# Causal attention with experts on one core: masked scores in two buffers, outputs in four, softmax inverses spread in fp32

## What is computed

```
xn = layernorm(x)
Q, K, V = heads(xn @ W_qkv)                 # 16 heads of 64
Q, K = rope on the first 32 of the 64 dims
scores = Q K^T, masked above the diagonal, / 8
attn = softmax(scores)
out = x + (attn V) @ W_o + experts(xn)      # top 2 of 8 experts and a skip; gelu between two products
```

## Time and profile before

| | us |
|---|---|
| median of 3 runs | 1490.87 (1490.24 to 1496.87) |
| the profiled execution | 1500.74, span 1499.0 |
| attention of the former samples, in the span | from about 128 to 690 |
| attention of the latter samples | from about 935 to the end |
| busy, share of the span | PE 84%, DVE 80%, ACT 75%, POOL 57% |

### The profile page before, as it was taken

How to read it: one execution, slowest core, us unless ns; L and a number is a source line. 1 busy time by engine, 2 the same in 40 slices (tenths; PEclk the granted TensorE clock), 3 DMA queues, 4 the chain that set the end, 5 groups by cost and what they waited for, 6 DMA issues and landing times.

```text
span 1499.0 us, 46446 instructions
## 1 busy us (share of the span) xinstructions
PE 1254.0 (84%) x15156; PEld 940.5 (63%) x15157; DVE 1195.7 (80%) x4018; ACT 1122.6 (75%) x3606; POOL 858.6 (57%) x1194
## 2 busy tenths in 40 slices
PE   1416999888888898895999999888888889888888
PEld 1404666666666666664889898566666666666666
DVE  5788877777777887783777777889988889889886
ACT  6415888877787787784878887878777777777786
POOL 3254777777777777773000000767777777666775
PEclk9757999999999999997999999999999999999999
DMA  9621433333333333333232322333333333333330
GB/s 290 204 56 38 101 73 73 74 72 72 74 72 74 72 80 79 75 83 111 72 88 84 87 84 75 77 80 79 80 82 92 91 84 80 89 91 89 85 80 27
DMA packets 115831, 130.12 MB, mean 87 GB/s; under 512 B 11568, under 2 KB 75312, under 8 KB 115376
## 3 DMA queue, kind: packets, MB, share of 16 engines
q1 hardware_dynamic: 107056, 110.26, 30.6%
q0 software_dynamic: 8576, 17.33, 3.8%
HBM read 28.85 MB, written 31.59 MB: 40 GB/s over the span
## 4 chain that ended last, share of the span: by engine, by line
PE 28%; DVE 22%; DMA 17%; POOL 16%; issue 13%; ACT 4%; POOLq 0%; DVEq 0%; SPq 0%; ACTq 0%
DMA sorted_x_dram<-stage,slots 17%; PE bank L1102 6%; PE bank L1103 6%; PE bank L1104 6%; DVE arena L956 4%; POOL sorted_x_dram L497 3%; POOL arena L476 3%; PE bank L1173 3%; DVE arena L919 2%; DVE arena L918 2%; POOL arena L456 2%; PE bank L1184 2%; POOL arena L457 2%; ACT probs L643 2%; PE bank L1211 2%
## 5 line engine op out<-in xcount | busy, mean ns | idle before, releaser
L643 ACT ACTIVATE probs<-arena,neg_max 128x128 f32<-128x128 f32 (+1 forms) x1024 | 452.3, 446 | 110.5 <-DVE neg_max L956 108.5
L956 DVE CUSTOM_DVE_ANT_0 arena<-bank,causal 128x128 f32<-128x128 f32 (+1 forms) x1024 | 302.3, 349 | 46.6 <-PE bank L1173 46.1
L507 POOL DMA_INDIRECT stage<-sorted_y_dram,slots x128 | 130.5, 1020 | 257.9 <-DVE arena L919 238.6
L1184 PE MATMUL bank<-ident,probs 128*128 128x128 f32 x1536 | 212.6, 275 | 13.5 <-ACT probsT L626 10.7
L633 ACT ACTIVATE o_whole<-bank 128x256 f32<-128x256 f32 x256 | 97.7, 382 | 151.5 <-PE bank L1195 85.2
L497 POOL DMA_INDIRECT sorted_x_dram<-stage,slots x128 | 133.3, 1041 | 128.6 <-DMA sorted_x_dram<-stage,slots 104.2
L1184 PEld LDWEIGHTS bank<-ident,probs 128*128 128x128 f32 x1536 | 177.2, 142 | 39.6 <-issue 18.4
L643 ACT ACTIVATION_READ_ACCUMULATOR probs<-arena,neg_max 128x1 f32 x1024 | 194.7, 190 | 0.0
L1102 PE MATMUL bank<-arena 128*128 (+1 forms) x864 | 183.2, 238 | 1.5 <-DVE arena L1076 1.5
L476 POOL TENSOR_TENSOR arena<-o_whole,arena 128x256 f16<-128x256 f32 x256 | 172.0, 672 | 21.0
L1103 PE MATMUL bank<-arena 128*128 (+1 forms) x864 | 182.7, 238 | 0.0
(11 more groups left out here) (152 smaller groups left out, 3258.8 us busy)
## 6 DMA issues: line engine op xcount, KB each, us to landing
arena<-arena SPq DMA_DIRECT2D x256, 256.0 KB, 3.8
arena<-sorted_x_dram SPq DMA_DIRECT2D x72, 128.0 KB, 2.2
sorted_y_dram<-stage SPq DMA_DIRECT2D x72, 128.0 KB, 1.8
sorted_x_dram<-arena SPq DMA_DIRECT2D x3, 2304.0 KB, 17.8
arena<-experts_dram SPq DMA_DIRECT2D x8, 512.0 KB, 5.6
out_dram<-acc SPq DMA_DIRECT2D x32, 128.0 KB
sorted_x_dram<-arena SPq DMA_DIRECT2D x1, 2368.0 KB, 19.1
sorted_x_dram<-stage,slots POOLq DMA_INDIRECT x128, 2.5
```

The costliest lines, as they stand in the source:

```text
L643: last = nc.scalar.activation(probs[:, s % 4, at:at + w], masked[:, s % 4, at:at + w], ACT.Exp, bias=neg_max[:, s % 4, t:t + 1], scale=-1. ...
L956: last = nc.vector.tensor_tensor_reduce(out=masked[:, (s + i) % 4, at:at + w], in0=SC[i][:, at:at + w], in1=causal[:, at:at + w], scale=1. ...
L1184: last = nc.tensor.transpose(TP[s % 2][:, k * P:(k + 1) * P], probs[:, s % 4, k * P:(k + 1) * P], ident[:])
```

## The change

- masked has two buffers, one for each head of a pair; the masks of a head wait until the exponentials of the same head of the pair before are done.
- o_whole has four buffers instead of two. o_copy waits for the products with v (pv_done) and for the split of the output four pairs back.
- invert runs once a pair and is a reciprocal alone; the row sums have four buffers instead of eight. turn_sums spreads the fp32 reciprocals by products with the fp32 identity, one for each row tile and head, and runs one period earlier (PV_LAG), after the units and before the transposes. The wait for o_scaled moves from attend to it. The factor 64 of the fp16 parts is gone.
- In the samples that have AHEAD units, except samples 0 and 16, "rest 0" of the sample after next moves from period 5 to the head of period 3, and within a period the units are ordered by table alone: AHEAD, then USUAL, then VALUES. So in period 7 "rest 1" comes before "v_low 1".

```diff
-AHEAD = ((5, "rest", 0), (6, "rope", 0), (7, "rest", 1))
+AHEAD = ((3, "rest", 0), (6, "rope", 0), (7, "rest", 1))
+AHEAD_OPENING = ((5, "rest", 0), (6, "rope", 0), (7, "rest", 1))
...
-T_LAG, PV_LAG, OUT_LAG, INV_LAG, SPLIT_LAG, BACK_LAG = 1, 2, 2, 3, 4, 2
+T_LAG, PV_LAG, OUT_LAG, COPY_LAG, SPLIT_LAG, BACK_LAG = 1, 2, 2, 3, 4, 2
-QUAD = 4
-SUMS = 2 * QUAD
+SUMS = 4
+OUTPUTS = 4
...
-    steps = [(p, kind, j, b if kind == "v_high" else b - 1 if kind == "y" else b + 1)
-             for p, kind, j in (OPENERS if b in (0, MID) else USUAL) if nearer or kind in ("v_high", "y")]
-    steps += [(p, kind, j, b + 2) for p, kind, j in AHEAD if further]
+    opening = b in (0, MID)
+    steps = [(p, kind, j, b + 2) for p, kind, j in (AHEAD_OPENING if opening else AHEAD) if further]
+    steps += [(p, kind, j, b if kind == "v_high" else b - 1 if kind == "y" else b + 1)
+              for p, kind, j in (OPENERS if opening else USUAL) if nearer or kind in ("v_high", "y")]
     steps += [(p, kind, j, b + 1) for p, kind, j in VALUES if nearer]
-    return sorted(steps, key=lambda step: (step[0], step[1] == "rest" or step[0] == 6 and step[1] == "v_low"))
+    return sorted(steps, key=lambda step: step[0])
...
-            pool.wait_ge(made, MADE - 1)
-            nc.gpsimd.tensor_copy(ident_h[:], ident[:]).then_inc(made, 1)
...
             def o_copy(J, j):
-                act.wait_ge(inv_turned, J + 1)
-                if not (isinstance(J, int) and J < 2):
-                    act.wait_ge(o_done, J - 1)
-                nc.scalar.activation(o_whole[:, j % 2, :], PV[j % 2], ACT.Copy).then_inc(o_out, 1)
+                act.wait_ge(pv_done, 2 * J + 2)
+                if J >= OUTPUTS:
+                    act.wait_ge(o_done, J - OUTPUTS + 1)
+                nc.scalar.activation(o_whole[:, J % OUTPUTS, :], PV[j % 2], ACT.Copy).then_inc(o_out, 1)
...
             def masks(b, s):
                 dve.wait_ge(s_ready, 8 * b + s // 2 + 1)
-                if not (b == 0 and s < 4):
-                    dve.wait_ge(exp_done, 16 * b + s - 2)
                 for i in range(2):
+                    if b > 0 or s > 0:
+                        dve.wait_ge(exp_done, 16 * b + s + i - 1)
...
-            def invert(N, n):
-                dve.wait_ge(exp_done, QUAD * N + QUAD)
...
+            def invert(J):
+                dve.wait_ge(exp_done, 2 * J + 2)
+                if J >= 2:
+                    dve.wait_ge(inv_turned, J - 1)
+                of = slice(J % 2 * 2, J % 2 * 2 + 2)
+                nc.vector.reciprocal(inv_total[:, of, :], total[:, of, :]).then_inc(inv_done, 1)
...
-                nc.vector.scalar_tensor_tensor(o_whole[:, j % 2, :], INV[j % 2], UNSCALE, o_whole[:, j % 2, :],
-                                               ALU.mult, ALU.mult).then_inc(o_scaled, 1)
+                nc.vector.tensor_tensor(o_whole[:, J % OUTPUTS, :], INV[j % 2], o_whole[:, J % OUTPUTS, :], ALU.mult).then_inc(o_scaled, 1)
...
-            def turn_sums(b, j):
...
+            def turn_sums(b, j, at):
+                pe.wait_ge(inv_done, 8 * b + j + 1)
                 if at == REOPEN and j == 0:
                     pe.wait_ge(y2_done, TILES)
                 if not (at == OPENING and j < 2):
                     pe.wait_ge(o_scaled, 8 * b + j - 1)
+                for t in range(TPS):
+                    for i in range(2):
+                        of = inv_total[:, j % 2 * 2 + i, t:t + 1].broadcast_to([P, DK])
+                        last = mm(INV[j % 2][64 * i:64 * i + 64, t * P:(t + 1) * P], of, ident[:], start=True, stop=True)
+                last.then_inc(inv_turned, 1)
...
             def sample(b, parity, at):
                 for p in range(PAIRS):
                     scores(b, 2 * p, parity, at == OPENING)
-                    then = past(b, p, INV_LAG)
-                    if then:
-                        turn_sums(*then)
                     for kind, j, of, u, psum in units_at(b, p):
                         unit(kind, j, of, of % 2, psum, bank_free(u))
+                    ended = past(b, p, PV_LAG)
+                    if ended:
+                        turn_sums(*ended, at)
                     then = past(b, p, T_LAG)
                     if then:
                         transposes(*then, then[0] == 0)
-                    then = past(b, p, PV_LAG)
-                    if then:
-                        attend(*then, at)
+                    if ended:
+                        attend(*ended)
```

More of the change, by code:

```diff
@@ L168, in attention_and_experts @@
         probs = sb("probs", [P, 4, PW], F32)
-        masked = view(MASKS, 4 * PW).rearrange("p (i n) -> p i n", i=4)
+        masked = view(MASKS, 2 * PW).rearrange("p (i n) -> p i n", i=2)
         probsT = sb("probsT", [P, 4, PW], F32)
@@ L173, in attention_and_experts @@
         inv_total = sb("inv_total", [P, SUMS, TPS], F32)
-        inv_parts = sb("inv_parts", [P, 2, SUMS, TPS], F16)
-        ident_h = sb("ident_h", [P, P], F16)
-        o_whole = sb("o_whole", [P, 2, SEQ], F32)
+        o_whole = sb("o_whole", [P, OUTPUTS, SEQ], F32)
         rot_q, rot_k = (view(ROT + i * 512, 2 * SEQ).rearrange("p (f t) -> p f t", f=2) for i in range(2))
@@ L220, in attention_and_experts @@
             "s_ready", "s_masked", "exp_done", "inv_done", "t_ready", "pv_done"))
-        inv_hi, inv_ready, inv_turned = (sem(n) for n in ("inv_hi", "inv_ready", "inv_turned"))
+        inv_turned = sem("inv_turned")
         t_out = [sem("t_out_dve"), sem("t_out_act")]
@@ L235, in attention_and_experts @@
         block = ctx.enter_context(nc.Block())
-        MADE = 7
+        MADE = 6
         ZEROED = 3 + E + 1 + 3
@@ L639, in exps @@
                     act.wait_ge(t_ready, G - 3)
-                if not (at_first and s < SUMS) and s % QUAD == 0:
-                    act.wait_ge(inv_done, G // QUAD - 1)
+                if G >= SUMS and s % 2 == 0:
+                    act.wait_ge(inv_done, G // 2 - 1)
                 for t, (at, w) in enumerate(((0, P), (P, 2 * P))):
-                    last = nc.scalar.activation(probs[:, s % 4, at:at + w], masked[:, s % 4, at:at + w], ACT.Exp,
+                    last = nc.scalar.activation(probs[:, s % 4, at:at + w], masked[:, s % 2, at:at + w], ACT.Exp,
                                                 bias=neg_max[:, s % 4, t:t + 1], scale=-1.0,
@@ L652, in sample @@
                     turned(past(b, p, OUT_LAG))
-                    then = past(b, p, INV_LAG)
+                    then = past(b, p, COPY_LAG)
                     if then:
@@ L1013, in sample @@
                     masks(b, 2 * p)
+                    then = past(b, p, 1)
+                    if then:
+                        invert(8 * then[0] + then[1])
                     for kind, j, of, u, psum in units_at(b, p):
@@ L1016, in sample @@
                             turn(j, u, psum, of)
-                    then = past(b, p, INV_LAG)
+                    then = past(b, p, COPY_LAG)
                     if then:
                         o_scale(8 * then[0] + then[1], then[1])
-                    then = past(b, p, 2)
-                    if then and p % 2 == 0:
-                        invert(4 * then[0] + then[1] // 2, then[1] // 2)
                     for kind, j, of, u, psum in due(b, p, 2):
@@ L1185, in transposes @@
                     last.then_inc(t_ready, 1)
-            def turn_sums(b, j):
-                if j % 2 == 0:
-                    pe.wait_ge(inv_ready, 4 * b + j // 2 + 1)
-                for t in range(TPS):
-                    for l in range(2):
-                        for i in range(2):
-                            of = inv_parts[:, l, 2 * j % SUMS + i, t:t + 1].broadcast_to([P, DK])
-                            last = mm(INV[j % 2][64 * i:64 * i + 64, t * P:(t + 1) * P], of, ident_h[:], start=(l == 0), stop=(l == 1))
-                last.then_inc(inv_turned, 1)
-            def attend(b, j, at):
-                if j % 4 == 0:
-                    pe.wait_ge(v_ready, 4 * b + (2 if j == 0 else 4))
+            def turn_sums(b, j, at):
+                pe.wait_ge(inv_done, 8 * b + j + 1)
                 if at == REOPEN and j == 0:
```

32 lines of the change are left out of this document (12 added, 20 removed).

## The result

The changed kernel takes 1615.3 us (median of 4 runs, 1607.61 to 1619.67) beside 1491.7 us of the kernel before on the same chip: ratio 1.0816, 95% interval 1.0767 to 1.0866. It is slower by 124 us where 25 were forecast, and the time lies outside the range (1478 to 1540 us). The profiled execution's span went from 1499.0 to 1612.2 us.

What follows compares the result with a forecast made beforehand. No engine was full: GpSimd's chain bound the former stage, a chain mostly through VectorE the latter. Ring +28.6 us in moved samples, less 3 us in unmoved, net +25.6 on 1490.9 gave 1516 us; range 1478 to 1540 us.

Steps and rivals of the forecast that it cites:

- the mask buffers: Two buffers for masked scores: forecast to cost nothing, at most 0.5 us in a few periods; rival that they bind, 0.05.
- the inverses' waits: Latter stage: waits on the inverses' fp16 parts (TensorE, 12.1 us in four samples) and before the output copy would go.
- the ring: Loop from q stack issue through 'y 0' to next issue: 36.2 us latter, 36.7 former, 28.6 us slower in all; chance 0.54.
- The clock: Rival: TensorE's pause before 'y 0' drops its clock for one period, up to 110 us more, up to 1620 us; chance 0.04.
- Five periods of TensorE: Ring term from 'y 0' to the end of next sample's period 1 scores: 5 x 4.08 = 20.4 us.
- The landing: Ring term from q stack issue until the stacks have landed: 7.2 us latter, 7.7 former, bounds 6.8 and 8.
- The masks of period 1: Ring term from scores of period 1 to their masks on VectorE: 0.9 us, bounds 0.1 and 1.5.
- Masks to next issue: Ring term from masks of period 1 to the next q stack issue: 6.3 us plus a reciprocal, 6.4 us.
- The unmoved samples: Samples without the moved unit (15, 30, 31 and openers): gain about 0.7 us each, 3 us together.
- relief wins: Rival: VectorE's 3.8 us and TensorE's 3 us of waits per sample disappear, about 1474 us; chance 0.17.

Runs made afterwards that it cites:

- the move alone: Kernel before with only the new placing of units ('rest 0' in period 3, order within a period by table): 1591.5 us, ratio 1.0634.
- its undoing: Changed kernel with 'rest 0' put back in period 5, all else of the change kept: 1491.0 us, ratio 0.9963.
- the run with a full clock: Changed kernel with 54 unused fp16 products added on TensorE ahead of the first unit of period 4: 1585.3 us, ratio 1.0579.
- the q stacks earlier: Changed kernel with GpSimd's low parts of the first two roped q tiles put ahead of the output split: 1583.2 us, ratio 1.0487.

## Why the prediction was wrong in size

What it said of the mechanism was right. ScalarE's rest_high waits once a sample, for the stacks; VectorE and TensorE wait behind it; the issues moved apart in the moved samples alone; the mask buffers are free; the inverses' waits went. It was the likeliest case, and the move alone (ratio 1.0634) and its undoing (0.9963) show that case. Two steps failed: the clock's price was no term of the ring's sum, and three terms of the sum were too small. The ring's 28.6 us were measured as 113; the difference has four parts.

- **The clock, 35 us (a rival that was wrongly set aside).** The prediction had the pause ("over 3 us per sample"), had the price of one period at the lower level, and gave the case 0.04 and no place in the range, because no row of before showed such a pause in an attention stage. That is a lack of evidence, not evidence against. It was no rival to the ring either: it follows from it. Whoever forecasts a new pause of TensorE has to carry the clock's price within the same case. The step that failed is that the chances treat ring and clock as cases that exclude each other.
- **Five periods of TensorE, 20 us.** Forecast 20.4 us, measured 21.13: 0.73 us in each of 27 rings. A period without a stall was to be 4.08 us, at most 4.18, and is 4.21. The fp32 spread was set at 0.55 us and is 0.59 (1213.02 - 1212.43), and a period with the fp16 spread is 3.82: so it is 0.39 us dearer where I took 0.22. I priced eight products from a row with two in each half, set them against the fp16 row, and added nothing for the switch from the units to them.
- **The landing, 17 us.** From the issue to rest_high I took 7.2 us (latter) and 7.7 (former); in the run with a full clock the means are 7.95 and 8.20, and single samples reach 9.8. That is 0.75 x 13 + 0.5 x 14. The bounds (6.8 and 8) were read from two samples; the later ends were in neither. Why some landings take 2 us longer than others was not tested.
- **The masks of period 1 in the former stage, 13 us.** Forecast 0.9 us after the scores in both stages. In the latter it is 0.92; in the former 1.8, over the bound of 1.5. VectorE's mix stands in front of them, and its operations are slower there than they were; the rows follow below.

The last three are 19.7 + 16.8 + 12.6 = 49.1 us, where 78.5 - 28.6 = 49.9 were to be explained: the terms close. "Masks to next issue" (6.4 us) was measured as 6.35.

The clock alone did not spoil the forecast: the run with a full clock, ratio 1.0579, lies outside the range too. Three terms were short by 0.5 to 0.9 us each, in a ring of 36, but the loss is only what that ring has over a sample of 35.4 us, and so it came out at little more than a third of what it is with a full clock.

The rival of the clock gave "up to 1620 us", and 1615.3 were measured. That is luck: it priced the clock at up to 110 us, which was 35, and took the ring's 28.6, which were 78.5. (Its own terms, 1516 + 110, give 1626.)

Two smaller points. The unmoved samples were to give 3 us; in the changed kernel the moved samples account for all of the difference, so they gave nothing. And "relief wins" named a true effect, 1.2 us a latter sample, which needs the ring open: it is what the runs with the unit in period 4 or 5 show, with the ratio 0.995.

## What to carry to other kernels

Before a unit is moved earlier, ask what its read-out overwrites and when the readers of that are done; if they are DMAs issued a little before, the wait lands in the queue of the reading engine, and everything queued behind it is late, not only the unit's own bank. Work out such a ring with a full clock, and then add the clock's price, if the ring makes TensorE pause: the two come together. And when one stage is bound by TensorE and the other by GpSimd, relief on VectorE and ScalarE gives little in either, while a copy moved from GpSimd to VectorE gave 0.8%. And where a forecast is the small difference of two long sums, a few tenths of a microsecond in each term decide it: the range has to be as wide as the sum of the terms' errors, times the number of rings.

## What the runs showed of the hardware

**The length of a pause did not decide the clock by itself.** In one sample of the changed kernel TensorE stood for 3.17 us before "y 0" (at 1210.99) and the granted clock stayed at 1.00; in the next it stood for 3.38 us and the clock was at 0.50 from 1247.0 on. But the first latter sample had 3.17 us too, and the clock was at 0.50 from 1059.3 on, for 3.4 us. With the q stacks earlier the pauses are shorter, and of the eight latter ones under 2.5 us five still came with such a stretch. One of them, first in TensorE's timeline and then in the windows (the clock is the third number from the end):

```profile
1226.02 0.29 PE L1094 MATMUL bank<-wvo_lo,arena 128*128 128x128 f16 x1 [2.13 <-DVE arena L922]
```

```profile
1226.00:1229.30 3.30, 3.28 (x30) 3.09 (x32) 2.76 (x13) 2.63 (x11) 1.53 (x3) 0.50 0.08 20
```

The products of "y 0" show the lower level, here after the pause of 3.38 us in the changed kernel:

```profile
1248.61 0.29 PE L1094 MATMUL bank<-wvo_lo,arena 128*128 128x128 f16 x1 [3.38 <-DVE arena L922]
...
1248.90 0.31 PE L1094 MATMUL bank<-wvo_lo,arena 128*128 128x128 f16 x1
1249.01 0.31 PE L1095 MATMUL bank<-wvo_hi,arena 128*128 128x128 f16 x1
```

They start 0.107 us apart; in the sample before, with a full clock, 0.056 (24 products and the switch in 1212.43 - 1210.99 = 1.44 us). Nearly the same pause costs nothing in one sample and over 2 us in the next. The Trainium skill (TensorE: Matmul & The Clock Gate, "Why this matters for your kernels") warns of pauses between bursts; the 20 of 27 rings with a fall agree with it, and the prediction should have given it more weight. What decides between two pauses of the same length no run here shows.

**VectorE's small operations beside GpSimd.** The group of mix (normalising the next rows of acc), 425 to 575 us, in the kernel before and then in the changed kernel:

```profile
L907 DVE TENSOR_SCALAR acc<-acc,small 128x128 f32<-128x128 f32 x8 | 2.4, 340 | 0.0
```

```profile
L905 DVE TENSOR_SCALAR acc<-acc,small 128x128 f32<-128x128 f32 x8 | 10.8, 1390 | 0.0
```

The same eight operations take four times as long, because they now fall beside other work. In one sample the pair of them took 2.71 us from 325.41, while GpSimd's rope_add ran from 325.53 (0.74 and 0.73 us) and its output split after it. The run with the q stacks earlier changed nothing but the order of GpSimd's work, and there the pair lies beside the issue of a scatter instead and is fast again:

```profile
L905 DVE TENSOR_SCALAR acc<-acc,small 128x128 f32<-128x128 f32 x8 | 2.4, 339 | 0.0
```

The new reciprocals are not stretched: mean 0.171 us over 32 of the latter stage. Both fit what the Trainium skill (SBUF — State Buffer, "Who interferes with whom") says of the port pair that VectorE and GpSimd share; that it is GpSimd's work beside mix that stretches it, that run shows; that it is the ports, it does not. The cost here is 0.9 us over the forecast in each of 14 rings.
